# Edge weights of two graph layers as K = 64 matmuls on the two halves of the array's rows

## The reference

```
h = silu(edge_scalars @ fcW1 / sqrt(8))         # (100000, 8) @ (8, 64)
w = h @ fcW2 / sqrt(64)                         # (100000, 64) @ (64, 192): the edge weights
wA, wB, wC, wD = w[:, :64], w[:, 64:128], w[:, 128:160], w[:, 160:192]
xs, xv = f_s[edge_src], f_v[edge_src]           # gathered rows of the source nodes
outA = wA * xs * y0;  outD = wD * einsum('eud,ed->eu', xv, y1) / sqrt(3)
outB = wB[:, :, None] * xs[:, :, None] * y1[:, None, :]
outC = wC[:, :, None] * xv * y0[:, :, None]
agg = segment_sum([outA, outD, outB, outC], edge_dst)
```

## Time and profile before

| | us |
|---|---|
| median of 3 runs | 9227.61 |
| lowest, highest run | 9198.25, 9258.36 |
| span of the profiled execution | 7226.5 |

### The profile page before, as it was taken

One profiled execution on the slowest core, in us unless ns is written; L12 is line 12 of the kernel. 1 busy time (PEld: TensorE's weight loads), 2 busy tenths in 40 slices (PEclk: granted clock), 3 DMA queues, 4 the chain that ended last, 5 costly groups with the idle time before them and its releaser, 6 DMA issues. The chain is left out here.

```text
span 7226.5 us, 182541 instructions
## 1 busy us (share of the span) xinstructions
PE 6569.0 (91%) x51671; PEld 5175.8 (72%) x51671; DVE 4888.2 (68%) x14416; ACT 3087.1 (43%) x8581; POOL 4427.4 (61%) x3934
## 2 busy tenths in 40 slices
PE   6999999799999857999999999999947879999998
PEld 3777778576666736878878777787836744777777
DVE  4666665476666545777777777777657975666665
ACT  2444443333333344666666666666530012333332
POOL 1777773277777216888877887878720011777772
PEclk9999997599999756889898888989778955999996
DMA  1222221222222213444444444444426701222221
GB/s 61 68 68 68 68 68 34 58 68 68 69 69 68 44 60 61 83 82 83 82 81 80 82 81 81 82 80 83 78 52 174 200 5 36 69 69 69 69 69 44
DMA packets 730807, 526.10 MB, mean 73 GB/s; under 512 B 244683, under 2 KB 677819, under 8 KB 730083
## 3 DMA queue, kind: packets, MB, share of 16 engines
q0 software_dynamic: 263424, 321.38, 22.1%
q1 hardware_dynamic: 467300, 203.73, 11.0%
HBM read 429.13 MB, written 95.55 MB: 73 GB/s over the span
## 5 line engine op out<-in xcount | busy, mean ns | idle before, releaser
L606 POOL DMA_INDIRECT l_edge_g<-node_table,l_edge_idx x2352 | 2281.7, 970 | 1124.3 <-issue 702.9
L649 PEld LDWEIGHTS l_edge_win_ps<-l_edge_hot,l_edge_prod 128*32 128x32 f32 (+2 forms) x23520 | 1515.3, 128 | 247.7 <-issue 170.4
L649 PE MATMUL l_edge_win_ps<-l_edge_hot,l_edge_prod 128*32 128x40 f32 (+2 forms) x23520 | 1620.9, 227 | 4.3 <-DVE sums_T L732 4.3
L1121 POOL DMA_INDIRECT att_g<-node_table,att_ends x784 | 1250.4, 1595 | 238.9 <-issue 238.6
L672 ACT ACTIVATE l_edge_gy<-l_edge_g,y 128x160 f32<-128x160 f32 x2352 | 811.7, 416 | 791.9 <-DMA l_edge_g<-node_table,l_edge_idx 789.3
L1114 POOL DMA_INDIRECT att_g<-node_table,att_ends x784 | 792.8, 1011 | 415.2 <-issue 281.3
L636 PE MATMUL l_edge_w_ps<-l_edge_wo,l_edge_h 128*128 128x384 f32 (+1 forms) x3136 | 907.1, 423 | 0.2 <-ACT l_edge_h L664 0.2
L664 ACT ACTIVATE l_edge_h<-l_edge_h_ps 128x256 f32<-128x256 f32 (+1 forms) x784 | 337.8, 431 | 1126.3 <-PE l_edge_h_ps L624 1076.6
L1141 PE MATMUL att_turn<-ident,sums_T 128*128 128x128 f32 (+1 forms) x4704 | 775.0, 309 | 30.1 <-ACT sums_T L1226 23.7
L636 PEld LDWEIGHTS l_edge_w_ps<-l_edge_wo,l_edge_h 128*128 128x128 f32 (+1 forms) x3136 | 536.8, 191 | 336.1 <-issue 171.7
L1226 ACT ACTIVATE sums_T<-att_turn 128x512 f32<-128x512 f32 (+1 forms) x1176 | 665.3, 591 | 216.7 <-PE att_turn L1141 211.8
(11 more groups left out here) (232 smaller groups left out, 11533.8 us busy)
## 6 DMA issues: line engine op xcount, KB each, us to landing
l_messages<-att_rows SPq DMA_DIRECT2D x196, 320.0 KB
sum_msg<-l_messages SPq DMA_DIRECT2D x196, 320.0 KB, 3.6
l_edge_g<-node_table,l_edge_idx POOLq DMA_INDIRECT x2352
att_g<-node_table,att_ends POOLq DMA_INDIRECT x1568
node_table<-l_rows SPq DMA_DIRECT2D x245, 80.0 KB, 1.6
att_ea<-in_edge_attr_T SPq DMA_DIRECT2D x196, 64.0 KB
l_scores<-att_score SPq DMA_DIRECT2D x784, 2.0 KB
l_edge_idx<-in_src_groups SPq DMA_DIRECT2D x588, 2.0 KB, 1.7
```

The costliest lines, as they stand in the source:

```text
L606: pool.indirect_dma_start(g[s][:, t, :], None, rows_of, bass.IndirectOffsetOnAxis(idx[s][:, t:t + 1], 0)).then_inc(fetched[s], 16)
L649: ins = nc.tensor.matmul(at, q[:, t, lo:lo + width], to[:, t, kinds, :], start=t == 0, stop=t == TG - 1)
L1121: pool.indirect_dma_start(g[s1][:, t, :], None, table[3], bass.IndirectOffsetOnAxis(ends[s1][:, TG + t:TG + t + 1], 0), compute_op=ALU.add ...
```

## The change

In layers 0 and 1 `wo` is no longer block-diagonal: both halves of its partitions hold the same 64 x 192 matrix. Each tile's edge weights come from a matmul of their own, K = 64, 192 columns, that reads its 64 rows of `h` and of `wo`. There are four such matmuls per group, and in program order they take the lower and the upper half of the rows in turn. The lower half writes tiles 0 and 1, the upper half tiles 2 and 3, so the two halves write to different banks of `w_ps`. On the host, the edge attributes are laid out so that the lower half holds tiles 0 and 1 of a group and the upper half tiles 2 and 3 (before: the even and the odd tiles). The memset of `wo` goes, in layer 3 too. In layer 3 (`HALVES` 1) the matmuls are the same as before.

```diff
-                wo = sbuf(ctx, f"{tag}_edge_wo", [HALVES * hid, HALVES * wn])
-                maps = [(wi, w_in), (wm, w_mid), (wo, w_out)] if w_mid else [(wi, w_in), (wo, w_out)]
+                wo = sbuf(ctx, f"{tag}_edge_wo", [HALVES * hid, wn])
+                blocks = [(wi, w_in), (wm, w_mid)] if w_mid else [(wi, w_in)]
...
-                        sp.wait_ge(w_zeroed, len(maps))
-                        for w, name in maps:
+                        sp.wait_ge(w_zeroed, len(blocks))
+                        for w, name in blocks:
                             rows, cols = A[name].shape
                             for n in range(HALVES):
                                 sp.dma_start(w[n * rows:(n + 1) * rows, n * cols:(n + 1) * cols], A[name]).then_inc(w_loaded, 16)
+                        for n in range(HALVES):
+                            sp.dma_start(wo[n * hid:(n + 1) * hid, :], A[w_out]).then_inc(w_loaded, 16)
...
                                 for n in range(TG // HALVES):
-                                    ins = nc.tensor.matmul(w_ps[s2][:, n * HALVES:(n + 1) * HALVES, 0:wn],
-                                                           h[last][s2][:, n * P:(n + 1) * P], wo[:, :])
+                                    for m in range(HALVES):
+                                        ins = nc.tensor.matmul(w_ps[s2][:, m * (TG // HALVES) + n, 0:wn],
+                                                               h[last][s2][m * hid:(m + 1) * hid, n * P:(n + 1) * P],
+                                                               wo[m * hid:(m + 1) * hid, :])
                                 ins.then_inc(weighed, 1)
...
-                        for w, _ in maps:
+                        for w, _ in blocks:
                             nc.vector.memset(w[:, :], 0.0).then_inc(w_zeroed, 1)
...
-    arrays["edge_attr_8_T"] = a.reshape(NG, TG // 2, 2, P, -1).transpose(2, 4, 0, 1, 3).reshape(2 * a.shape[1], -1)
+    arrays["edge_attr_8_T"] = a.reshape(NG, 2, TG // 2, P, -1).transpose(1, 4, 0, 2, 3).reshape(2 * a.shape[1], -1)
```

More of the change, by code:

```diff
@@ L574, in edge_pass @@
                 last = layers - 1
-                W_LOAD = 16 * HALVES * len(maps)
+                W_LOAD = 16 * HALVES * (len(blocks) + 1)
                 def half(s, r):
```

## The result

| | median, us | lowest, highest | runs |
|---|---|---|---|
| before | 9231.56 | 9198.25, 9258.36 | 4 |
| changed | 9330.90 | 9322.17, 9381.41 | 4 |

The ratio is 1.0127, with a 95% interval of 1.0085 to 1.0168; the medians differ by 99 us. The changed kernel is slower, where the forecast was 9214.6 us. (A ratio here is estimated from all runs of both kernels, and need not be that of the two medians.) The profiled execution took 9330.25 us and its span is 9328.4 us, so only 2 us lie outside a span. The trace of before has a span of 7226.5 us and therefore belongs to an execution of about 7228 us.

What follows compares the result with a forecast made beforehand. The prediction took layer 0 as bound by PE and POOL together, layer 1 by POOL's gathers. Terms of -12, 0 and -1 us gave -13 us, carried over to the median of 9227.6 us: 9214.6 us, range 9160 to 9290.

Steps and rivals of the forecast that it cites:

- predicted 0.86: Layer 0's edge-weight matmuls: eight passes run in pairs, 0.65 us plus 0.21 us around them, against 1.29 us before.
- predicted 0.08: Layer 0, PE: added time per step for changing row arrangement ahead of the edge-weight matmuls, 0.08 us.
- sign of error: A granted clock below 0.98 in layer 0 or layer 1 was listed as showing the forecast wrong.
- predicted 5.054: Layer 0's step, set by POOL's gathers, falls from 5.115 to 5.054 us; between 5.03 and 5.09 us had chance 0.50.
- the 13 us: Whole kernel's forecast gain: 12 us from layer 0, 0 from layer 1, 1 us from loading without the memset.
- the 12 us that I had: Layer 0's gain over its 196 steps, from a step of 5.054 instead of 5.115 us.
- Rivals A to D: A POOL unchanged, 9227 us, 0.19; B POOL free, 9194, 0.09; C halves serial, ≤9307, 0.06; D gathers lengthened, 9359, 0.04.
- PE's step was to be 4.76 us: Layer 0: PE gains 0.35 us per step and could do one in 4.76 us instead of 5.11.
- their 0.21 us: Time around the paired edge-weight passes, taken from `weigh` in attention; assumed to include the second change of arrangement.
- those 2001 us: Difference between the profiled span, 7226.5 us, and the runs' median, 9227.6 us, carried over as unchanged.
- Rival F: Timed runs have a slower PE than the profile, so shorter L636 saves at most 430 us, 8800 us; chance 0.07.
- rival E: Layers 0 and 1: thinner L636 lets PE's clock fall, a step loses about a tenth, +200 us, 9430; chance 0.05.

Runs made afterwards that it cites:

- split: Before with each edge-weight matmul cut in two of 192 columns, K = 128: 7207.06 us (0.9998) on chip 1, 9464.39 us (1.0036) on chip 3.
- thin: Changed kernel, but each edge-weight matmul takes all 128 rows and only 96 of 192 columns: 1.0003 of before on chip 13, 9301.60 us (1.0068) on chip 11.
- loops exchanged: Changed kernel with the two loops around L639 exchanged, one half's two matmuls before the other's: 7202.63 us (0.9990) on chip 1, 9503.10 us (1.0077) on chip 3.
- filler: Changed kernel plus one unused 128-row, 256-column matmul per step in layers 0 and 1: 1.0051 of before on chip 1, 1.0054 on chip 5, 1.0074 on chip 3.

## Why the prediction was wrong

**What held, on chips like that of the trace.** POOL and PE were both full in layer 0, and POOL sets the step once PE is shorter. L639 takes 705.13 - 704.28 = 0.85 us (predicted 0.86), with 0.09 us ahead of it (predicted 0.08; L632 is followed by L639 after 0.63 us, not 0.54). ACT waits 498.0 us for gathers in layer 0, as it did in layer 1; DVE's wait of 116.6 us is gone; gathers take 963 ns and 192.2 us lie before them; PE has a gap. The clock of layer 1, 0.94, is below the 0.98 that I had named as a sign of error; it cost nothing there. Layer 0's step is 5.07 us (predicted 5.054, before 5.115) and layer 1's 5.07. The two ratios on such chips, 0.9991 and 0.9993, hold the 13 us (0.9982) inside their intervals, and hold zero as well. Layer 0's gain over the whole pass is 6 us (1001 to 995), half of the 12 us that I had, so part of the term was too large, and the total can't tell. Rivals A to D are refuted there by the steps and L639, not by the total. The Trainium skill ("TensorEngine Tiling (Array Packing)", Key Properties) says that changing the tiling mode drains TensorE, and the trace agrees that it costs something: 0.09 us ahead, and nothing ahead in the split and thin kernels, whose matmuls all take 128 rows there (0.54 us after the second map, as before).

**A term that was mis-sized.** PE's step was to be 4.76 us. On chip 3, with the loops exchanged, PE runs some steps at full clock with nothing to wait for:

```profile
518.12 0.69 PE L626 MATMUL l_edge_h_ps<-l_edge_ea,l_edge_wi 16*128 16x256 f32 x2
518.75 0.70 PE L632 MATMUL l_edge_h_ps<-l_edge_h,l_edge_wm 128*128 128x256 f32 x2
519.37 0.93 PE L639 MATMUL l_edge_w_ps<-l_edge_wo,l_edge_h 64*128 64x192 f32 x8
520.23 2.81 PE L653 MATMUL l_edge_win_ps<-l_edge_hot,l_edge_prod 128*96 128x40 f32 x40
522.98 0.69 PE L626 MATMUL l_edge_h_ps<-l_edge_ea,l_edge_wi 16*128 16x256 f32 x2
```

That is 4.86 us. L653 takes 2.75 us to the next L626, against 2.66 in the earlier trace rows: the second change of arrangement stands behind the pairs, 0.09 us, and not inside their 0.21 us. PE gains 0.25 us, not 0.35. The result doesn't hang on this: where PE had room, POOL set the step either way, and where it had none, the saving was outweighed by the clock.

**The step that failed.** "I take those 2001 us as unchanged". A difference of 28% between span and median was carried as a constant, and the trace taken as typical of the timed runs. Those have standstills and half of the clock for much of the time, and PE sets the step. Rival F said this and got the sign wrong, since it kept the clock fixed; rival E said what the clock does and kept the chip quiet. The case was the two together, and neither had a chance of more than 0.07.

**The balance, from chip 3.** Length of a stage times its mean clock, over 196 steps, is the full-clock time that a step uses. In layer 1 before uses 1453 x 0.805 / 196 = 5.97 us, the exchanged kernel 1494 x 0.662 / 196 = 5.05 us: 15.4% less. But the clock is 17.8% lower (0.846 / 0.822 = 1.029, the ratio of the two lengths, as it must be). In layer 0 it is 6.31 and 5.74 us, 9% less, with a clock 12% lower (0.850 and 0.748). The saving is real in both, and the trace shows roughly where it comes from. In layer 0, 0.25 us of the 0.57 is the shorter step at full clock (5.11 and 4.86), and the standstills counted above, weighted with the clock, go from 1.17 to 0.85 us per step, 0.32 us. In layer 1 it is 0.46 us (4.68 and 4.22) and 0.51 us (1.34 to 0.83), together 0.97 for the 0.92 of the balance. The clock takes back more than all of it. By how much is a measurement; no rule here gives its size. The Trainium skill ("TensorE: Matmul & The Clock Gate", Part 1) says that "the default state is throttled, and activity releases the throttle"; the longer stretches at half clock after each standstill agree in direction. The filler is the test of it: more work brings the clock back part of the way (0.805 and 0.737), but it costs its own time and doesn't pay (1.0074 on chip 3, where the kernel with its loops exchanged has 1.0077).

**What stays open.** Why PE stands still on chips 3, 8 and 11 and on that of the first result, and not on chips 1, 5 and 13; each of the six chips was used once, so a lasting trait of the chip and its condition at that hour are not told apart. Why the clock loses more than the work saved. The changed kernel itself was not run on chip 3: there the kernel with its loops exchanged stands for it. How the loss divides between the layers with one layer changed at a time. No version was found that beats before on chips with standstills; on the others the changed kernel equals it.

## What to carry over

Set the span of a profile against the median of the timed runs before anything else: if they differ, the trace is of another regime, and each term has to be priced in both. A matmul made shorter is no gain by itself where PE's clock is not full: ask what clock the engine gets once the stage has changed. A busy share or the length of a step doesn't give it; a run with the same part made thinner, on a chip of the slower kind, does. Where the engine is not the bound, the same cut costs nothing and brings nothing.

## What the runs showed of the hardware

- The same kernel takes 7205 to 7209 us on three chips and 9231 to 9420 us on three others, with one core in use. The granted clock over the span is 0.87 to 0.88 on the first and 0.73 to 0.76 on the others.
- On the latter PE stands still without a wait, mostly for 0.6 to 0.8 or 1.3 to 1.5 us from one matmul's start to the next, in changed and unchanged passes alike (L649 of before on chip 3: 547.1 us of "issue").
- It does so above all at the full clock: in layer 0 of before on chip 3, from 200 to 1600 us, 211 of 245 standstills begin at 2.4 GHz, which holds for 982 of the 1400 us. All 69 falls of the clock in that pass come during a standstill or at most 2.3 us after one.
- Without any standstill the clock falls as well: in layer 1 of the changed kernel on chip 5 it is 0.94, where before has 0.99.
- Float32 matmuls of K = 64 on the two halves overlap whether or not the program alternates them: L639 takes 0.85 and 0.86 us.
- PE at 2.4 GHz needs 1.30 us (layer 0) or 1.40 us (layer 1) for eight passes of 192 columns with K = 128, in the split kernel, and 0.85 us with K = 64 in pairs; at 1.2 GHz, in layer 1, 2.72 and 1.58 us.
